# Early edge loads and a first count whose high one-hots come from GpSimd and ScalarE, in a four-layer graph network on one core

## The reference, cut to what matters

```python
src = jnp.concatenate([_s, _d, _loop]); dst = jnp.concatenate([_d, _s, _loop])
x = _layernorm(x + _L0_gnn_ref(x, edge_attr_3, edge_weight1, ..., edge_index))
x = _layernorm(x + _L1_gnn_ref(x, ..., src, dst))
x = _layernorm(x + _L2_gnn_ref(x, edge_index, edge_attr_16, ...))
x = _layernorm(x + _L3_gnn_ref(x, edge_index, edge_weight, ...))
# inside each: out = segment_sum(weight * rows[one_end], other_end, num_segments=n)
```

## Time and profile before

| | us |
|---|---|
| median of 3 runs (9075.75 to 9084.97) | 9079.56 |
| span of the profiled execution, core 0 | 9077.3 |
| constants, until its end | about 8.3 |
| first block of load_src: start to the first product | 8.3 to 27.2 |
| count loop on TensorE, first product to the last | 27.2 to 149.5 |
| second block begins | 153.4 |

### The profile page before, as it was taken

The page is one execution under the profiler, slowest core; times in us unless marked ns, Lnnn a source line. Parts: engine busy times, 40 slices in busy tenths (PEclk is TensorE's granted clock), DMA queues, the critical chain, the costliest instruction groups (busy, mean ns, idle before and its releaser), DMA issues. The chain is left out here.

```text
span 9077.3 us, 124550 instructions
## 1 busy us (share of the span) xinstructions
PE 5529.8 (61%) x32289; PEld 4875.7 (54%) x32289; DVE 5121.2 (56%) x14751; ACT 2279.7 (25%) x4226; POOL 6148.2 (68%) x6249
## 2 busy tenths in 40 slices
PE   6777757777639997036777755777733333433334
PEld 5666657777627775026676645666623333333333
DVE  7777654444489997045777743445554444444445
ACT  0111111111127775023444433444320000000000
POOL 2777767777627777747777727777537777577774
PEclk9556558888757776567888865555555555655556
DMA  1000007777627765025555533444312222221111
GB/s 33 13 12 12 10 11 211 210 210 210 179 55 162 163 163 115 2 64 141 139 139 137 130 38 79 80 80 81 58 39 53 53 53 53 50 52 52 52 52 47
DMA packets 993339, 792.54 MB, mean 87 GB/s; under 512 B 426646, under 2 KB 868378, under 8 KB 992720
## 3 DMA queue, kind: packets, MB, share of 16 engines
q1 hardware_dynamic: 536692, 373.45, 17.0%
q0 software_dynamic: 211680, 354.89, 16.1%
q10 hardware_dynamic: 244600, 60.13, 3.0%
HBM read 693.22 MB, written 94.60 MB: 87 GB/s over the span
## 5 line engine op out<-in xcount | busy, mean ns | idle before, releaser
L1426 PE MATMUL sum_ps_sum<-sum_hot,sum_msg 128*128 128x128 f32 x3528 | 841.2, 431 | 1420.1 <-DVE acc L1395 1362.7
L1426 PEld LDWEIGHTS sum_ps_sum<-sum_hot,sum_msg 128*128 128x128 f32 x3528 | 770.7, 330 | 1490.7 <-DVE acc L1395 1421.5
L514 POOL DMA_INDIRECT payload_src<-load_src_pay_slot,load_src_at_i x882 | 873.2, 990 | 439.7 <-issue 270.1
L641 POOL DMA_INDIRECT payload_dst<-place_dst_pay,place_dst_at_i x882 | 926.2, 1050 | 352.4 <-issue 304.5
L1370 POOL DMA_INDIRECT sum_rows<-x_table,dst_other x882 | 844.4, 957 | 442.5 <-issue 268.5
L1370 POOL DMA_INDIRECT sum_rows<-conv_table,dst_other x882 | 843.9, 957 | 334.0 <-issue 268.5
L1495 POOL DMA_INDIRECT attend_rows<-xl_table,dst_other x882 | 867.9, 984 | 295.7 <-issue 267.3
L1495 POOL DMA_INDIRECT attend_rows<-h_table,dst_other x882 | 858.0, 973 | 303.3 <-issue 268.3
L1045 POOL DMA_INDIRECT scores_rows<-kv_table,scores_idx x882 | 834.4, 946 | 308.5 <-issue 248.1
L1568 PE MATMUL attend_ps_sum<-attend_hot,attend_msg 128*128 128x128 f32 x3528 | 690.8, 366 | 372.7 <-DVE acc L1730 327.0
L1555 PE MATMUL attend_ps_x<-attend_win,attend_hot_t 128*128 128x136 f32 (+1 forms) x3528 | 770.9, 327 | 228.1 <-DMA attend_rows<-xl_table,dst_other 166.3
(11 more groups left out here) (437 smaller groups left out, 13710.0 us busy)
## 6 DMA issues: line engine op xcount, KB each, us to landing
attend_win<-xr_table SPq DMA_DIRECT2D x882, 68.0 KB
scores_win<-q_table ACTq DMA_DIRECT2D x882, 64.0 KB
spill<-scores_rows SPq DMA_DIRECT2D x126, 448.0 KB
place_dst_key_all<-key_rows_dst SPq DMA_DIRECT2D x126, 448.0 KB
place_dst_rows<-spill SPq DMA_DIRECT2D x126, 448.0 KB
attend_rel_all<-rel_flat_dst SPq DMA_DIRECT2D x252, 224.0 KB
place_dst_low_all<-low_rows_dst SPq DMA_DIRECT2D x126, 224.0 KB
payload_src<-load_src_pay_slot,load_src_at_i POOLq DMA_INDIRECT x882
```

Of the source, the lines that this page charges most:

```text
L514: pool.indirect_dma_start(o.payload, bass.IndirectOffsetOnAxis(ap=at_i[:, s, j:j + 1].bitcast(U32), axis=0), pay_slot[:, s, j, :], None).t ...
L641: pool.indirect_dma_start(o.payload, bass.IndirectOffsetOnAxis(ap=at_i[:, t:t + 1].bitcast(U32), axis=0), pay[:, t, :], None).then_inc(sca ...
L1426: mm = pe.matmul(ps_sum[:, n, j, :], msg[:, n, j, :], hot[:, n, j, :], start=True, stop=True)
```

## The change

The four edge loads move from load_src to the constants stage, each with a semaphore of its own (`raw_in`). ScalarE's payload copies wait each for its own column, and ScalarE takes over `hi_bf`. VectorE waits for the key column alone before it splits it; the split of the other end moves behind VectorE's part of the count loop. In the loop VectorE writes only the low one-hot. The high one is made in three steps: GpSimd subtracts the group's high parts from the column numbers into `hi_off` (two buffers), ScalarE squares it into `one_hi`, and ScalarE turns 0 into 1 and the rest into 0 with a second activation in place. TensorE waits for both engines. The bits of the split go to another part of `acc`, since the raw columns are still being read. The second block is not changed.

```diff
--- before.py
+++ after.py
@@ -148,7 +148,7 @@
             self.has_end = sb("has_end", [1, R])
 
 
-def constants(nc, keep):
+def constants(nc, keep, loads):
     class C:
         pass
     c = C()
@@ -167,6 +167,11 @@
         made, ones_ready, ident_ready, pick_ready, bf_ready = (
             st.sem(n) for n in ("made", "ones", "ident", "pick_ready", "bf"))
         with nc.Block() as block:
+            @block.sync
+            def _(sp):
+                for buf, src, arrived in loads:
+                    sp.dma_start(buf, src).then_inc(arrived, 16)
+
             @block.gpsimd
             def _(pool):
                 pool.memset(c.ident[:], 0.0).then_inc(ident_ready, 1)
@@ -217,12 +222,12 @@
     return c
 
 
-def sort_edges(nc, c, o, key_d, other_d, weight_d, real_d, counts, count_next, weights, spare, turns, x, tables, fold):
+def sort_edges(nc, c, o, raw, raw_in, counts, count_next, weights, spare, turns, x, tables, fold):
 
 
     with stage(nc, f"load_{o.name}") as st:
-        key, other, bits = (spare[:, n * T:(n + 1) * T].bitcast(I32) for n in range(3))
-        weight, real = (spare[:, n * T:(n + 1) * T] for n in (3, 4))
+        key, other, weight, real = raw
+        bits = spare[:, 4 * T:5 * T].bitcast(I32)
 
         lo_bf, hi, hi_bf = (st.sb(n, [P, T], BF16) for n in ("lo_bf", "hi", "hi_bf"))
         pay = st.sb("pay", [P, T, 4])
@@ -238,7 +243,10 @@
         ps_counts, ps_sums = st.ps("counts", [P, 512]), st.ps("sums", [P, 512])
         ps_lo, ps_key = st.ps("lo", [P, 8, P]), st.ps("key", [P, 8, P])
         weights_turned = st.sem("weights_turned")
-        loaded, weights_in, steps, paid, split = (st.sem(n) for n in ("loaded", "weights_in", "steps", "paid", "split"))
+        weights_in, steps, paid = (st.sem(n) for n in ("weights_in", "steps", "paid"))
+        hi_ready, products_ready = st.sem("hi_ready"), st.sem("products_ready")
+        hi_off = st.sb("hi_off", [P, 2, HB, G], BF16)
+        hi_differed, hi_squared = st.sem("hi_differed"), st.sem("hi_squared")
         cleared, hot_ready, hot_used, counted, copied, summed = (
             st.sem(n) for n in ("cleared", "hot_ready", "hot_used", "counted", "copied", "summed"))
 
@@ -246,21 +254,29 @@
         with nc.Block() as block:
             @block.sync
             def _(sp):
-                for buf, src in ((key, key_d), (other, other_d), (weight, weight_d), (real, real_d)):
-                    sp.dma_start(buf[:], src).then_inc(loaded, 16)
                 with nc.allow_non_contiguous_dma(reason="vectors across partitions, once"):
                     for dst, src in weights:
                         sp.dma_start(dst, src).then_inc(weights_in, 16)
-                sp.wait_ge(loaded, 64)
                 sp.wait_ge(weights_in, 16 * len(weights))
 
             @block.scalar
             def _(act):
-                act.wait_ge(loaded, 64)
-                for f, buf in enumerate((key, other, weight, real)):
-                    act.copy(pay[:, :, f], buf[:]).then_inc(paid, 1)
-                act.wait_ge(paid, 4)
+                for f, (buf, arrived) in enumerate(zip((key, other, weight, real), raw_in)):
+                    act.wait_ge(arrived, 16)
+                    act.copy(pay[:, :, f], buf).then_inc(paid, 1)
+                act.wait_ge(products_ready, 1)
+                act.activation(hi_bf[:], hi[:], ACT.Copy, scale=float(P)).then_inc(paid, 1)
+                act.wait_ge(paid, 5)
                 if True:
+                    with act.Fori(0, R // 2) as i:
+                        for s in range(2):
+                            gi = 2 * i + s
+                            act.wait_ge(hi_differed, gi + 1)
+                            act.wait_ge(hot_used, gi + 1)
+                            act.activation(one_hi[:, s], hi_off[:, s], ACT.Square).then_inc(hi_squared, 1)
+                            act.wait_ge(hi_squared, gi + 3)
+                            act.activation(one_hi[:, s], one_hi[:, s], ACT.Relu, bias=c.ones[:, 0:1],
+                                           scale=-1.0).then_inc(hi_ready, 1)
                     act.wait_ge(counted, 1)
                     act.copy(counts[:], ps_counts[:, 0:HB]).then_inc(copied, 1)
                     act.wait_ge(weights_turned, 1)
@@ -274,18 +290,12 @@
                 link = Chain(dve, steps)
                 dve.memset(zero[:], 0.0).then_inc(cleared, 1)
                 link(dve.tensor_copy(column_g[:], over_tiles(c.column[:], G)))
-                dve.wait_ge(loaded, 64)
-                link(dve.tensor_single_scalar(bits[:], key[:], P - 1, ALU.bitwise_and))
-                link(dve.tensor_copy(lo_bf[:], bits[:]))
-                link(dve.tensor_single_scalar(bits[:], key[:], 7, ALU.arith_shift_right))
-                link(dve.tensor_copy(hi[:], bits[:]))
-                link(dve.tensor_scalar(hi_bf[:], hi[:], float(P), None, ALU.mult))
-                dve.wait_ge(paid, 4)
-                if True:
-                    link(dve.tensor_single_scalar(bits[:], other[:], P - 1, ALU.bitwise_and))
-                    link(dve.tensor_copy(next_lo[:], bits[:]))
-                    link(dve.tensor_single_scalar(bits[:], other[:], 7, ALU.arith_shift_right))
-                    link(dve.tensor_copy(next_hi[:], bits[:]))
+                dve.wait_ge(raw_in[0], 16)
+                link(dve.tensor_single_scalar(bits, key, P - 1, ALU.bitwise_and))
+                link(dve.tensor_copy(lo_bf[:], bits))
+                link(dve.tensor_single_scalar(bits, key, 7, ALU.arith_shift_right))
+                link(dve.tensor_copy(hi[:], bits))
+                dve.sem_inc(products_ready, 1)
                 if True:
                     dve.sem_inc(hot_used, 2)
                     with dve.Fori(0, R // 2) as i:
@@ -294,15 +304,28 @@
                             dve.wait_ge(hot_used, gi + 1)
                             dve.tensor_tensor(one_lo[:, s], column_g[:], per_tile(group(lo_bf, gi), P),
                                       ALU.is_equal).then_inc(hot_ready, 1)
-                            dve.tensor_tensor(one_hi[:, s], column_g[:, 0:HB], per_tile(group(hi, gi), HB),
-                                      ALU.is_equal).then_inc(hot_ready, 1)
-                    dve.wait_ge(hot_ready, 2 * R)
-
+                    dve.wait_ge(hot_ready, R)
+                dve.wait_ge(raw_in[1], 16)
+                link(dve.tensor_single_scalar(bits, other, P - 1, ALU.bitwise_and))
+                link(dve.tensor_copy(next_lo[:], bits))
+                link(dve.tensor_single_scalar(bits, other, 7, ALU.arith_shift_right))
+                link(dve.tensor_copy(next_hi[:], bits))
                 dve.wait_ge(summed, 1)
                 link(dve.tensor_copy(totals[:], ps_sums[:, 64:64 + HB]))
                 link(dve.tensor_tensor_scan(upto[:], c.ones[:, 0:HB], totals[:], 0.0, ALU.mult, ALU.add))
                 link(dve.tensor_tensor(upto[:], upto[:], totals[:], ALU.subtract))
                 link(dve.tensor_tensor(first[:], upto[:], ps_sums[:, 0:HB], ALU.add))
+
+            @block.gpsimd
+            def _(pool):
+                pool.sem_inc(hi_squared, 2)
+                pool.wait_ge(products_ready, 1)
+                with pool.Fori(0, R // 2) as i:
+                    for s in range(2):
+                        gi = 2 * i + s
+                        pool.wait_ge(hi_squared, gi + 1)
+                        pool.tensor_tensor(hi_off[:, s], column_g[:, 0:HB], per_tile(group(hi, gi), HB),
+                                           ALU.subtract).then_inc(hi_differed, 1)
 
             @block.tensor
             def _(pe):
@@ -312,7 +335,8 @@
                     with pe.Fori(0, R // 2) as i:
                         for s in range(2):
                             gi = 2 * i + s
-                            pe.wait_ge(hot_ready, 2 * gi + 2)
+                            pe.wait_ge(hot_ready, gi + 1)
+                            pe.wait_ge(hi_ready, gi + 1)
                             for j in range(G):
                                 mm = pe.matmul(ps_counts[:, 0:HB], one_lo[:, s, :, j], one_hi[:, s, :, j],
                                                start=False, stop=True, skip_group_check=True)
@@ -2555,8 +2579,11 @@
         sb = lambda n, s, dt=F32: keep.enter_context(nc.sbuf_tensor(n, s, dt))
         dram = lambda n, s: nc.dram_tensor(n, s, F32).ap()
         by_dst = Order(nc, "dst", keep, keep, True)
-        c = constants(nc, keep)
         x, acc = sb("x_nodes", [P, NB, D]), sb("acc", [P, NP])
+        raw = [acc[:, n * T:(n + 1) * T] for n in range(4)]
+        raw[0], raw[1] = raw[0].bitcast(I32), raw[1].bitcast(I32)
+        raw_in = [nc.alloc_semaphore(f"raw_in{n}") for n in range(4)]
+        c = constants(nc, keep, list(zip(raw, (src, dst, length, real), raw_in)))
         src_counts, dst_counts = sb("src_counts", [P, HB]), sb("dst_counts", [P, HB])
         spill = dram("spill", [R * P, G * D])
         by_dst.real = None
@@ -2585,7 +2612,7 @@
```

(2 more changed lines are left out.)

## The result

The changed kernel takes 9114.5 us (median of 5 runs, 9109.04 to 9121.64) against 9079.56 (5 runs, 9075.75 to 9086.2): 1.0038 of the time before, 95% interval 1.0027 to 1.0048, slower by 35 us. The profiled execution has a span of 9112.2 us against 9077.3.

A forecast was written before the change was run, and what follows sets the result against it. VectorE bounds the loop before; after, VectorE and GpSimd alternate at the ports: 0.50 + 0.80, with turns 1.33 us a group; 125 x 1.33 - 130.5 = +35.7, 9113.0 profiled, median 9115.3, range 9080 to 9153.

The forecast's parts named there:

- The direction and the mechanism: First block's loop: VectorE's low one-hot and GpSimd's difference go one after the other at the SBUF ports; slower, chance 0.62.
- The first rival: Loop: ports do not meet, ScalarE is the bound at 1.06 us a group, +2.0 us, 9081.6; chance 0.14.
- The second: Loop: operations go strictly one behind the other, 1.62 us a group, +72.0 us, 9151.6; chance 0.14.
- the third: Loop: ports do not meet, ScalarE is cheaper, GpSimd bounds at 0.89 us a group, -19.3 us, 9060.3; chance 0.06.
- 0.19 + 0.13: Loop: the parts of VectorE's and GpSimd's own operation times, in us, taken to lie under the wait for the port.
- The start: Before the loop: earlier loads let TensorE start at about 18.2 against 27.18, 9.0 us won.
- c: First block's loop: the time of one group, predicted at 1.33 us, with a range from 1.20 to 1.45.
- the few hundredths for turns: Loop: allowance for turns in which neither VectorE nor GpSimd has its next instruction ready, raising 1.30 to 1.33 us a group.
- another price of the bf16 difference as a sign of being wrong: Loop: the prediction is wrong if GpSimd's bf16 difference is priced otherwise than its f32 ones; it took 0.93 us.
- 125c - 130.5: End of the loop: change in us of when TensorE's last seven products start, over 125 groups; predicted +35.7.
- the whole rest shift by what the first block shifts: Behind the first block: everything later moves by the first block's shift, predicted +35.7 us.
- hidden, as said: Behind the loop: the other end's split, 2.6 us, lies beside about 3 us of other work; without cover it costs 2.6.

The follow-up runs named there:

- experiment 3: Changed kernel, but VectorE's low one-hot reads the column numbers from PSUM, so it has one SBUF input: 1.05 us a group, 1.0001 of the kernel before.
- experiment 4: Against early loads alone, GpSimd adds one unread difference per group: 1.49 us a group; with a fill instead: 0.97.
- eight timed rows of the table: Runs of the changed kernel and its follow-up variants, timed against the kernel before on the same chip: ratios 0.9974 to 1.0037.
- early loads alone: Changed kernel, but VectorE writes both one-hots again, GpSimd and ScalarE idle in the loop: 0.97 us a group, 0.9984 and 0.9993 of the kernel before.
- mixed kernels: Early loads, PSUM column numbers, VectorE makes even groups' high one-hots, GpSimd and ScalarE odd ones: 0.9998; square ahead 0.9998; three buffers 0.9974 of the kernel before.

## Why the prediction came out as it did, point by point

**The direction and the mechanism.** Slower, because VectorE's low one-hot and GpSimd's difference exclude each other: shown. The operand's place (experiment 3) switches it off, and the difference alone (experiment 4) switches it on. The first rival (no meeting, ScalarE at 1.06, +2.0) is what experiment 3 built: 1.05 a group and +0.6. The second (nothing overlaps, 1.62) and the third (faster) did not come: with the measured prices nothing overlapping would be 0.69 + 0.82 = 1.51, and 1.21 leaves an overlap of 0.30, where the prediction had 0.19 + 0.13.

**The start.** TensorE at 18.2, measured 18.39; `hi_bf` 0.91, measured 0.95; square and second activation 0.46 and 0.58, measured 0.495 and 0.587.

**The step whose size was off.** c was 1.33 and is 1.210. The term is GpSimd's difference: 0.93, drawn from 640 and 896 f32 elements, and it takes 0.77 to 0.82 alone. With 0.82 the prediction's own sum is 0.50 + 0.69 = 1.19, and with the few hundredths for turns 1.22. The 0.12 a group are 15 us of the sum: 125c - 130.5 gives +20.8 with the measured c, and +20.8 is measured at the first scatter. So the sum for the first block was 15 us too long, and the last products started at 169.6 where the prediction looked for them near 184. It had named another price of the bf16 difference as a sign of being wrong; that sign came, with 0.82 for 0.93, and was too small to change the direction.

**The total.** It was predicted at 9115.3 and is 9114.5, and this closeness is not earned. The prediction let "the whole rest shift by what the first block shifts"; the rest added 14.1 us on the profiled pair, nearly what the sum had too much. Without that the median would be near 9100, which is still slower by 0.23% and inside the stated range.

**Behind the loop.** The split of the other end runs from 169.33 to 171.92, and the totals follow at 171.95, 2.34 behind the start of the last group (2.36 before): hidden, as said, with nothing to spare.

**What stays open.** Whether the 14.1 us are the change's. For it: on the first chip the lowest of five runs after is 22.8 us above the highest of five before, and the interval, 24.5 to 43.6 us, does not reach 20.8. Against it: no instruction behind the first block differs, the shift does not sit at one place, and on the other chips two profiles of the same changed kernel end 40 us apart (spans of 11,654.3 and 11,693.8) with first blocks alike. The eight timed rows of the table say little more: the difference of the medians, less that of the first scatter against 168.9, lies between -5 and +12 us, with the changed kernel at +5; for the early loads alone it is -5 and +6. This takes the 168.9 of one chip for all four. Neither the semaphores nor the addresses were varied on the first chip, so no cause is named.

## What to carry to other kernels

Before work goes to GpSimd beside VectorE, count the SBUF inputs: where VectorE's instruction has two and GpSimd's reads SBUF, their times add up but for some 0.3 us a pair, and a busy VectorE gets slower though work was taken from it; one input in PSUM or a fill on GpSimd cost nothing here. Two inputs are not shown to be the only case: in the kernel before, a GpSimd operation beside a VectorE copy with one SBUF input took 2.35 instead of 1.54, and no experiment varied that. A step that moves from 0.36 us on one engine to three steps on two others has to be priced on its slowest new engine first: ScalarE's pair alone, at 1.05, was already above the 0.97 that it should relieve. And a faster engine shows the next chain: two buffers held two of the mixed kernels at 0.97 to 1.02, and a third one, with a longer pass, let 0.79 through.

## What the runs showed of the hardware that was not expected

VectorE reads bf16 column numbers from PSUM as fast as from SBUF: 691 and 690 ns for 128x896, 352 and 359 for 128x350. GpSimd's two-input difference costs 0.77 to 0.82 at 128x350 bf16, less than the line through its f32 rows (0.93). A recorded duration holds the wait for the port, on GpSimd too: its difference stands at 1240 ns in the loop and ran in 820. And one program ran at 9,080 us on one chip and at 11,650 to 11,685 on others, behind the first block. In the two profiles of the kernel before, 2,489 of the 2,598 us between the spans lie between the first and the last indirect issue of the seven stages that have them; why was not looked into.
